# Contexts transposed by VectorE out of their PSUM bank, without ScalarE's copy

## What is computed

```
for layer in (0, 1):
    h = layernorm(x) * (1 + ca) + sa
    q, k, v = heads(h @ Wq), heads(h @ Wk), heads(h @ Wv)     # 16 heads of 16
    scores = (q @ k.T masked, + alibi in layer 0) / 4
    w = softmax(scores)
    ctx = w @ v                                               # 1024 x 256
    x = x + ga * (ctx @ Wo + b)
    x = x + gb * ffn(layernorm(x) * (1 + cb) + sb)
```

## Time and profile before

| | us |
|---|---|
| median of 3 runs | 2815.2 |
| lowest, highest | 2811.31, 2816.49 |
| the profiled execution | 2814.14 |
| its span, first to last instruction | 2812.1 |
| PE busy (matmuls) | 2448.3 |
| DVE busy | 2278.1 |
| ACT busy | 1711.8 |
| POOL busy | 850.1 |
| mean granted clock of PE, as a share of full speed | 0.951 |

### The profile page before, as it was taken

The page is one execution under the profiler, slowest core; times in us unless marked ns, Lnnn a source line. Parts: engine busy times, 40 slices in busy tenths (PEclk is TensorE's granted clock), DMA queues, the critical chain, the costliest instruction groups (busy, mean ns, idle before and its releaser), DMA issues.

```text
span 2812.1 us, 54982 instructions
## 1 busy us (share of the span) xinstructions
PE 2448.3 (87%) x18968; PEld 1041.3 (37%) x18968; DVE 2278.1 (81%) x7158; ACT 1711.8 (61%) x3458; POOL 850.1 (30%) x954
## 2 busy tenths in 40 slices
PE   6798877988989898988989989998989889887586
PEld 4223434323334333343434333443333434333223
DVE  4899747899987998978988898878989788962872
ACT  3286563676765576665766656755766657665164
POOL 3211351234222432225232342224322252225121
PEclk8799988999999999999999999999999999998789
DMA  7511125113312222322322123222232223001200
GB/s 232 149 47 31 37 72 146 53 35 98 118 49 83 78 79 91 90 69 76 106 68 80 57 90 100 77 77 73 76 93 89 69 80 104 22 30 61 86 19 16
DMA packets 142393, 218.28 MB, mean 78 GB/s; under 512 B 21190, under 2 KB 62556, under 8 KB 142052
## 3 DMA queue, kind: packets, MB, share of 16 engines
q1 hardware_dynamic: 142120, 214.77, 24.7%
HBM read 137.87 MB, written 77.89 MB: 77 GB/s over the span
## 4 chain that ended last, share of the span: by engine, by line
PE 55%; DVE 31%; ACT 7%; issue 4%; POOL 2%; DMA 1%; SPq 0%; DVEq 0%; ACTq 0%; POOLq 0%
PE ctx_ps L1627 12%; PE big L1608 11%; PE big L1545 11%; DVE small L1371 10%; PE small L1586 8%; PE big L1534 8%; DVE mx L1369 6%; PE big L1659 4%; ACT probs L1146 4%; ACT xn L1195 2%; DVE region L1439 2%; DVE stats L1314 2%; PE big L1642 2%; DVE mx L1371 2%; DVE region L1477 1%
## 5 line engine op out<-in xcount | busy, mean ns | idle before, releaser
L1146 ACT ACTIVATE probs<-big 128x512 f32<-128x512 f32 (+2 forms) x2560 | 1221.2, 563 | 509.2 <-PE big L1608 500.2
L1371 DVE CUSTOM_DVE_ANT_0 small<-small,mask 128x128 f32<-128x128 f32 (+3 forms) x2048 | 941.3, 518 | 158.2 <-PE small L1586 151.8
L1608 PE MATMUL big<-stack_q,stack_k 64*128 64x512 f16 (+3 forms) x6144 | 709.2, 331 | 65.5 <-ACT probs L1146 40.5
L1056 POOL TENSOR_SCALAR_AFFINE_SELECT probs<-probs 128x512 f32<-128x512 f32 x512 | 329.5, 653 | 1347.3 <-ACT probs L1146 1347.0
L1369 DVE TENSOR_REDUCE mx<-small 128x1 f32<-128x512 f32 x1024 | 652.3, 681 | 53.3 <-PE small L1586 45.9
L1627 PE MATMUL ctx_ps<-probs,v_ones 128*17 128x512 f32 (+3 forms) x6144 | 634.8, 501 | 8.5 <-POOL probs L1056 7.6
L1586 PE MATMUL small<-stack_k,stack_q 64*128 64x512 f16 (+3 forms) x3072 | 466.2, 341 | 195.0 <-DVE mx L1371 110.6
L1608 PEld LDWEIGHTS big<-stack_q,stack_k 64*128 64x128 f16 x6144 | 250.4, 95 | 491.9 <-issue 297.7
L1586 PEld LDWEIGHTS small<-stack_k,stack_q 64*128 64x128 f16 x3072 | 122.1, 94 | 693.2 <-DVE mx L1371 347.1
L1371 DVE DVE_READ_ACCUMULATOR2_ANT mx<- 128x1 f32 x2048 | 283.8, 139 | 0.0
L1534 PE MATMUL big<-hT,w_qkv 128*128 128x512 f32 x512 | 259.6, 623 | 0.3 <-issue 0.2
(11 more groups left out here) (93 smaller groups left out, 1913.3 us busy)
## 6 DMA issues: line engine op xcount, KB each, us to landing
image<-region SPq DMA_DIRECT2D x192, 256.0 KB
stack_q<-image SPq DMA_DIRECT2D x64, 512.0 KB, 3.7
stack_k<-image SPq DMA_DIRECT2D x64, 512.0 KB, 4.6
lo_dram<-region SPq DMA_DIRECT2D x64, 256.0 KB
w_qkv<-wqkv SPq DMA_DIRECT2D x16, 768.0 KB, 5.1
x_res<-x SPq DMA_DIRECT2D x32, 256.0 KB, 3.2
stack_q<-lo_dram SPq DMA_DIRECT2D x128, 64.0 KB, 3.9
stack_k<-lo_dram SPq DMA_DIRECT2D x128, 64.0 KB, 4.6
```

Source lines behind the costliest of these rows:

```text
L1056: g.affine_select(out=diag, in_=diag, compare_op=ALU.is_ge, fill=0.0, base=0, pattern=[[0, GH], [1, P]], channel_multiplier=-1).then_inc(m ...
L1146: s.activation(probs[:, n % HELD, heads, q0:], big[:, at.slot(turn), 0:len(pairs) * width] .rearrange("p (h q) -> p h q", h=len(pairs)), A ...
L1371: last = v.tensor_tensor_reduce(out=held, in0=held, in1=mask[:, BANK - width:], scale=1.0, scalar=3.0 * NEG, op0=ALU.add, op1=ALU.max, acc ...
L1608: last = te.matmul(big[:, at.slot(at.turn() + parity), j * width:(j + 1) * width], stack_k[rows, c, g * PAIR_N + pair, kt * P:(kt + 1) * P ...
```

## The change

The item `save` becomes DVE's: it waits for the block's last context, as ACT's copy did, and for part 2 of the block before, which reads `ctx_b`, and transposes `ctx_ps` straight into `ctx_b`. It raises `ctx_saved`, for which PE waits. Part 0 of `norm`, ACT's copy, the buffer `ctx_u` and the semaphore `u_read` are gone. The planner is told that `save` costs 640 on DVE, and four of its constants change, so the whole order is made anew.

```
-QK_LAGS = (0.0, 0.7758, 1.7394, 3.0788, 5.9576)
+QK_LAGS = (0.0, 0.3955, 1.7394, 3.0788, 5.9576)
...
-AHEAD = {"score": 0.0124, "context": 0.0085, "max": 0.7639, "pre": 1.5711, "post": 0.0063}
+AHEAD = {"score": 0.0191, "context": 0.0085, "max": 0.7639, "pre": 1.5711, "post": 0.0063}
...
-SEEN, DMA_NS = 232.7037, 466.9094
+SEEN, DMA_NS = 232.7037, 687.3960
...
-FIRST_FEED, FEED_WAIT = {"max": 216.0, "score": 430.0}, 300.0000
+FIRST_FEED, FEED_WAIT = {"max": 216.0, "score": 430.0}, 195.3801
...
         if item[0] == "save":
-            model.ready["saved"] = model.ready["copied", *item[1:4]] = model.run("ACT", model.at("context"), 490)
+            model.ready["saved"] = model.ready["norm"] = model.run("DVE", model.at("context"), 640)
         elif item[0] == "norm":
-            ready = model.at(("copied", *item[1:4])) if item[4] == 0 else model.at("norm")
-            model.ready["norm"] = model.run("DVE", ready, (640, 200, 330, 640)[item[4]], 110)
+            model.ready["norm"] = model.run("DVE", model.at("norm"), (0, 200, 330, 640)[item[4]], 110)
...
-                later.append((lambda end=end: end, "ACT", ("save", u, g, blk)))
-                for part in range(4 if g % 2 else 3):
+                later.append((lambda end=end: end, "DVE", ("save", u, g, blk)))
+                for part in range(1, 4 if g % 2 else 3):
...
-                elif kind == "save":
-                    _, _, g, blk = item
-                    n = BLOCK_AT[unit, g, blk]
-
-                    act.wait_ge(pv_done, context_number(unit, g, blk, (blk + 1) * 4 - 1) + 1 + HELD)
-                    act.wait_ge(u_read, n + 1)
-                    s.activation(ctx_u[:], ctx_ps[:], ACT.Copy).then_inc(ctx_saved, 1)
...
+                elif kind == "save":
+                    _, _, g, blk = item
+
+                    dve.wait_ge(pv_done, context_number(unit, g, blk, (blk + 1) * 4 - 1) + 1 + HELD)
+                    dve.wait_ge(v_chain, scaled_at[0])
+                    v.transpose(ctx_b[:], ctx_ps[:]).then_inc(ctx_saved, 1)
...
-                    if part == 0:
-
+                    if part == 1:
                         dve.wait_ge(ctx_saved, n)
-                        dve.wait_ge(v_chain, scaled_at[0])
-                        v.transpose(ctx_b[:], ctx_u[:]).then_inc(u_read, 1)
-                    elif part == 1:
-                        dve.wait_ge(u_read, n)
                         mark(v.reciprocal(own[:, :, DH:DH + 1], own[:, :, DH:DH + 1]))
```

More of the change, by code:

```diff
@@ L589, in plan @@
                 end = model.ready["context"]
-                later.append((lambda end=end: end, "ACT", ("save", u, g, blk)))
-                for part in range(4 if g % 2 else 3):
-                    later.append((lambda u=u, g=g, blk=blk, part=part: model.ready.get(("copied", u, g, blk), 1e18) if part == 0
-                                  else model.at("norm"), "DVE", ("norm", u, g, blk, part)))
+                later.append((lambda end=end: end, "DVE", ("save", u, g, blk)))
+                for part in range(1, 4 if g % 2 else 3):
+                    later.append((lambda: model.at("norm"), "DVE", ("norm", u, g, blk, part)))
     return out
@@ L741, in adaln_program @@
         probs = sb("probs", [P, HELD, GH, BANK])
-        ctx_u = sb("ctx_u", [P, BANK])
         ctx_b = sb("ctx_b", [P, BANK])
@@ L841, in adaln_program @@
         ctx_saved = sem("ctx_saved")
-        u_read = sem("u_read")
         ctx_ready = sem("ctx_ready")
@@ L1228, in _ @@
             dve.sem_inc(ctx_saved, 1)
-            dve.sem_inc(u_read, 1)
             dve.wait_ge(c_in, 32)
```

## The result

The median is 2831.7 us (2828.0 to 2833.9, 4 runs) against 2813.8 us (2811.3 to 2816.5, 4 runs) for the kernel before. The ratio is 1.0062, with a 95% interval of 1.0049 to 1.0075. So the change makes the kernel **slower by 0.6%, about 17.5 us**. The forecast was 2808 us, faster. The time is near that of rival B (2828 us) and just inside the outermost range (2785 to 2832), but beyond the forecast's own range (2799 to 2818).

A forecast was written before the change was run, and what follows sets the result against it. PE and DVE were taken to share the bound, ACT third. 2814.1 - 6.3 + 0 + 5.5 - 4.5 - 0.6 = 2808.2, about 2808 us; own range 2799 to 2818, outermost 2785 to 2832.

The forecast's parts named there:

- rival B: DVE's queue takes the copy's place at block ends; full 39 us of waits, +21 instead of +5.5: 2828 us, chance 0.23.
- Term 3: At block ends the bank of `ctx_ps` comes free later, through DVE's queue: +5.5 us, bounds 0 and 21.
- The overlay: New release rule laid over the old trace's 127 block ends: 44 late, 39 us together; 25 of them carry 33 us.
- the cut for the new order: At block ends, PE's work between blocks grows in the new order, leaving 20 us gross of the 39 us.
- Term 2: DVE's transpose reads PSUM instead of SBUF, 128 times at about 700 ns: 0 us, from -2.4 to +1.7.
- rival D: The new order takes an eighth (23 us) off PE's 181.1 us at matmuls for DVE's maxima: 2790 us, chance 0.13.
- Term 4: New order on every engine, fewer long PE stretches without items DVE takes: -4.5 us, range widened by 10 both sides.
- this sign: DVE's waits for PE's `small` (L1371) fall below 151.8 us if the new order's gain is right; unchanged if not.
- term 1: 128 copies, 78.9 us of busy time, go from ACT; some 8% on the path: -6.3 us, bounds 0 and 20.
- its mark: Profile sign for the copies gone from ACT: its busy time down by 79 us to about 1633.
- term 5: At the kernel's end, without the last copy, DVE's transpose and the projection behind it start some 0.6 us sooner: -0.6 us.
- Its test: Waits of `ctx_ps` loads and matmuls for DVE's `ctx_b`: 10 to 25 us expected; over 40 would mean rival B.

The follow-up runs named there:

- the old order: Every item in its place as in the kernel before; run with DVE transposing out of the bank where ACT's copy stood, no copy: 2835.3 us, ratio 1.0092.
- the later release: Kernel before, its order unchanged, no copy; DVE transposes the bank, and so frees it, at the old place of `norm`'s part 0: 2889.1 us, ratio 1.0280.
- 25 worst blocks: Kernel before, its order; at 25 block ends called late by over 0.5 us DVE frees the bank at `save`, copy at 103: 2823.5 us, ratio 1.0055.
- 36 blocks: Kernel before, its order; 36 blocks transposed straight at `save`, 48 straight at the old place, 44 by copy: 2817.0 us, 10.7 slower than without the 36.
- five other orders: Kernel before with four new constants 2863.1 us, one 2834.8; kernel after with old constants 2841.7, transpose priced 705 ns 2877.3, bank told 500 ns later 2883.2.
- the two runs meant to part these: Kernel after with ACT's copy and release back; DVE's transpose of the copy at `save`: 2886.4 us, or just ahead of the reciprocal: 2876.2 us.

## Why the prediction was wrong

**Term 3 failed: the cost of the bank that comes free later was put at 5.5 us, too low by its last two factors.** The overlay of the new rule on the old trace was right: 39 us called, 34.4 measured in the old order; 33 called at 25 places, 32.3 measured; the later release gave 123.3 us in 78 places. So was the cut for the new order: 20 us gross, 21.9 measured in the kernel after. Then the text took half of it away as time that PE "would have lost a moment later", and 55% of the rest, which leaves 27%. The runs have 42 to 48% (25 worst blocks, where the queue place counts too) and 60% to two thirds (the later release). With these shares the 21.9 us cost 9 to 15 us and not 5.5. The timeline at 1092 us shows how, at one place: PE's wait holds the `max` matmuls behind it, the contexts behind the stand run at the lower clock, and DVE, the other bound, stands next. A share of the chain isn't the share of a stall in which both bounds stop.

**A term was missing.** Term 2 priced how long the transpose takes (0; measured 5 ns more, 0.6 us in all) and not where it stands. The early place costs 10.7 us for 36 blocks without any wait for the bank. Nothing in the sum had this (term 2 stands in it as 0), though the text says that nothing stands on DVE any more between the last context and the transpose, and it used the 181.1 us of waits for maxima only in rival D, as something to gain.

**Term 4 had the wrong sign as a term.** The forecast gave the new order -4.5 us against the time before. It regains at most 4 to 8 us of the 26 that the release costs in the old order, almost none of it in the steady period, and it has 28 us more idle for the maxima than the kernel before, and no run shows it better than the old order for a kernel with the copy (with the new constants alone that is 53 us slower). DVE's waits for L1371 did fall, 151.8 to 102.6 us, as the text wanted for term 4; but those for L1369's maxima rose (137.3 us, 45.9 of idle before), so this sign said nothing. The 10 us given to what a reordering may move beside were far too few: five other orders came out 10 to 75 us worse.

**Right, as far as the runs can tell:** term 1 (6.3; 2 to 7 or less by the runs). The figure that the prediction gave as its mark was wrong, though: ACT's busy time fell by 56 us and not by 79 (1655.7, not 1633). Its other operations took no longer (the exponentials 1222.1 us, 1221.2 before). Neighbours on ACT overlap in the trace: its rows add up to 1754 us before, 43 more than its busy time, and to 1677 after, 22 more. So a copy held ACT for 0.44 us net of such overlap and not for 0.62. PE's idle behind the exponentials fell to 34.3. The transpose's time was right: 705 ns, in the range of 680 to 715. What the Trainium skill ("VectorE: DVE Perf Modes", section "The TRN2 errata") would add for a PSUM source, an estimated 65 ns, isn't there: 705 beside 700 in the two kernels, 708 beside 698 in one kernel, and in the run with the copy kept and the early place all 128 out of SBUF took 705. Right was also term 5, in the last rows of the kernel after, which answer to the earlier trace rows:

```profile
2799.62 1.00 PE L1616 MATMUL ctx_ps<-probs,v_ones 128*17 128x256 f32 x16 [1.00 <-POOL probs L1052]
...
2800.69 0.72 DVE L1384 STREAM_TRANSPOSE ctx_b<-ctx_ps 128x512 f32<-128x512 f32 x1 [13.76 <-PE ctx_ps L1616]
```

The transpose starts 0.07 us after the last context ends; before, the copy's 0.60 us lay between.

**Rival B**, DVE's queue in the copy's place, named the mechanism and came near the time (2828 us). The nearness is in part luck: its sum has the full 39 us of waits for the bank, where 21.9 came, and nothing for the transpose's place or the order, which stand in for the rest. Its test, over 40 us of waits for `ctx_b`, doesn't decide: the loads waited 44.0 us (the row in which the copy had 11.3), the matmuls idled 21.9, in part the same time. The test looked for the cost under the new wait's name; in the new order more of it sits under the maxima.

One slip of the text: the earlier trace rows shows as its first pair the second of the late block ends, at 166 us, and not the one at 149.92 of which the text speaks. The point is the same there: the next contexts start before DVE's transpose of the block.

**What stays open** is the split of the kernel after's own 17.5 us. From the shares above, 2 to 7 us gained on ACT and 9 to 15 us for the bank leave some 5 to 15 us for the transpose's place in the queue and for the order, and the two runs meant to part these were inconclusive. How much of it is waiting and how much a lower clock is open too (below). Which property of an order makes it 50 us worse wasn't found either.

## What to carry to other kernels

Before giving a release to another engine, lay it over the old trace (the waits it called here came place by place), price them at the share of a stall in which both bounds stop (here 42% to two thirds), and price the instruction's earlier place in its new queue apart, by what is pushed back behind it. A copy on an engine that isn't the bound, which frees a scarce bank promptly, is cheap (128 copies, 79 us of work, for 2 to 7 us of time); take it away only where the busy engine comes by early enough on its own. An order tuned for one table of costs loses tens of microseconds under another, and a truer price in the planner doesn't by itself make a better one.

## What the runs showed of the hardware

**Same matmuls, more busy time at a lower mean clock.** All kernels issue the same 18968 matmuls. The kernel before has them in 2448.3 us at a mean granted clock of 0.951, the kernel after in 2448.2 at 0.949; some of the re-ordered ones need 20 to 29 us more. The engine line of the kernel whose planner was told of a later release:

```profile
PE 2477.4 (86%) x18968; PEld 1042.7 (36%) x18968; DVE 2269.9 (79%) x7158; ACT 1651.5 (57%) x3330; POOL 845.7 (29%) x954
```

and what the trace gives as its clock:

```profile
core 0: 2881.3 us, clock 0.939
```

The old kernel with new constants has 2468.9 us at 0.943, and the new order with copy and late transpose 2468.0 at 0.941. In the traces the granted clock has two levels, 2.4 GHz and half of it: in the kernel before PE is at the lower one for 277 us in 39 stretches, in the new order with copy and late transpose for 341 us in 54. So of what these three lose, some 20 to 29 us is the same work done slower, and it comes on top of the waits. It isn't the sum of PE's idle time that decides: the run with the later release idles PE for 435 us (its span of 2883.5 less 2448.7 busy), more than any of these, and has 0.948 and the busy time of the kernel before. Which idle lowers the clock wasn't found. In the two profiled executions of the change this plays no part: the busy time is the same to 0.1 us. It may in the medians: the four executions of the kernel after have 0.947 to 0.950, and the two at 0.947 are its slowest (2833.4 and 2833.9 us; 2828.0 at 0.950). Within one kernel time and clock go together as well: of the 52 executions of the kernel before beside the experiments, the ten at 0.950 took 2813.5 to 2817.0 us, and the one at 0.958 took 2799.5. An estimate from these is 2 us for each 0.001.

**A scaling that took longer.** DVE's multiplication into `ctx_n` took 557 ns on average before and 629 after, 9.2 us over 128, with the same operands; that is DVE's 8 us of added busy time. The median is the same, 424 and 425 ns. What grew is the number of long ones, over 700 ns: 22 before with a mean of 1179 ns, 39 after with 1095. POOL is at work for 1.05 us of such a long one on average in the kernel before and for 1.04 us in the kernel after, and for 0.04 us of a short one in both. In none of the kernels did a multiplication take over 700 ns without POOL at work for more than half of it. One such place in the kernel after:

```profile
1020.58 5.16 POOL L1072 TENSOR_TENSOR x_res<-x_res,bias_bc 128x512 f32<-128x512 f32 x4 [4.51 <-ACT xn L1184]
...
1020.61 0.71 DVE L1384 STREAM_TRANSPOSE ctx_b<-ctx_ps 128x512 f32<-128x512 f32 x1
...
1023.36 1.26 DVE L1395 TENSOR_TENSOR ctx_n<-ctx_b 128x256 f32<-128x256 f32 x1
```

The transpose beside the same work of POOL keeps its time (0.71 us); the multiplication takes 1.26. So it goes with the order, which puts it beside POOL's work more or less often: 616 to 629 ns on average in the four kernels with exactly the new order, 540 to 568 in those with the old one, and 500 to 576 in others. No run moved POOL's work alone.
